# The order of two TensorE steps, convolution and second spread of B, in the middle stage of a vision network kernel

## The reference

```python
xw = windows_of_8x8(layernorm_over_channels(x)) + pos     # 64 steps, 64 channels
xz = seq @ W_in;  x, z = split(xz)                        # 128 + 128 channels
x  = silu(causal_conv1d(x, conv_w, 4 taps) + conv_b)
dt, B, C = split(x @ W_xproj)                             # 4, 16, 16 columns
dt = softplus(dt @ W_dt + b_dt)
h  = exp(dt * A) * h + dt * u * B      # scan over 64 steps, 128 channels x 16 states
y  = (h * C summed over states) + u * Dp
out = (y * silu(z)) @ W_out
```

## Time and profile before

| what | value |
|---|---|
| median of 3 runs | 8367.6 us |
| profiled execution | 8380.57 us |
| its span | 8378.7 us |
| VectorE busy, share of span | 81% |
| GpSimd busy | 62% |
| TensorE matmuls busy | 74% |
| ScalarE busy | 52% |
| granted TensorE clock, mean | 0.83 of full |

### The profile page before, as it was taken

The page is one execution under the profiler, slowest core; times in us unless marked ns, Lnnn a source line. Parts: engine busy times, 40 slices in busy tenths (PEclk is TensorE's granted clock), DMA queues, the critical chain, the costliest instruction groups (busy, mean ns, idle before and its releaser), DMA issues. The chain is left out here.

```text
span 8378.7 us, 102295 instructions
## 1 busy us (share of the span) xinstructions
PE 6196.3 (74%) x30542; PEld 2432.9 (29%) x30542; DVE 6788.1 (81%) x7950; ACT 4334.6 (52%) x5972; POOL 5194.6 (62%) x1732
## 2 busy tenths in 40 slices
PE   6888888888885777777777777777777777767737
PEld 3444444444441222222222222222222222222213
DVE  3555555555555999999999999999999999999976
ACT  1222222222223666666666666666666666666642
POOL 0000000000005999999999999999999999999950
PEclk8988898998986888888888888888888888888867
DMA  1111111111113556556556656655655665565567
GB/s 31 44 40 44 38 46 38 42 42 40 44 37 133 191 190 210 199 190 206 200 189 203 207 189 200 206 190 192 205 200 189 203 207 189 198 208 191 187 165 261
DMA packets 514970, 1253.48 MB, mean 150 GB/s; under 512 B 170313, under 2 KB 172525, under 8 KB 513901
## 3 DMA queue, kind: packets, MB, share of 16 engines
q1 hardware_dynamic: 514092, 1249.20, 45.8%
q10 hardware_dynamic: 320, 3.21, 0.2%
q0 software_dynamic: 512, 0.53, 0.0%
HBM read 943.30 MB, written 231.21 MB: 140 GB/s over the span
## 5 line engine op out<-in xcount | busy, mean ns | idle before, releaser
L1186 DVE TENSOR_TENSOR_SCAN b_h<-b_a,b_h 128x448 f32<-128x448 f32 x3584 | 3668.0, 1070 | 101.0 <-ACT b_a L1115 94.7
L1024 POOL TENSOR_TENSOR b_h<-b_h,b_ct 128x1792 f32<-128x1792 f32 x896 | 3570.3, 3987 | 278.4 <-DVE b_h L1186 265.6
L1115 ACT ACTIVATE b_a<-b_dts,decay 128x441 f32<-128x441 f32 x3584 | 2225.7, 629 | 1587.5 <-DVE b_h L1186 1560.0
L1036 POOL MEMSET b_seq<- 128x938 f32 x2 | 1.7, 880 | 2497.0 <-POOLq L799 2497.0
L1176 DVE TENSOR_TENSOR b_h<-b_dus,b_b 128x896 f32<-128x896 f32 x1344 | 1429.9, 1064 | 62.4 <-DMA b_dus<-d_dtu 61.1
L1283 PE MATMUL b_b<-b_rows,spread_b 16*128 16x512 f32 (+1 forms) x1792 | 565.2, 651 | 891.1 <-DVE b_h L1176 890.1
L1010 POOL TENSOR_TENSOR b_h<-b_dus,b_bt 128x896 f32<-128x896 f32 x448 | 933.3, 2083 | 44.6 <-DMA b_bt<-d_rows 27.8
L1291 PE MATMUL b_y<-b_h,fold 128*32 128x512 f32 (+1 forms) x7168 | 953.5, 659 | 8.1 <-POOL b_h L1024 8.1
L496 DVE TENSOR_TENSOR a_xg<-a_xd,a_pb 128x784 f32<-128x784 f32 x512 | 495.0, 967 | 511.7 <-PE a_pb L610 509.6
L1252 PE MATMUL b_w<-b_seq,w_conv 128*128 128x384 f32 (+1 forms) x896 | 560.1, 789 | 12.6 <-DMA b_seq<-b_seq 12.6
L1244 PE MATMUL b_w<-b_u,wx 128*64 128x512 f32 x448 | 361.3, 962 | 211.2 <-DVE b_dt L1208 211.2
(11 more groups left out here) (226 smaller groups left out, 8470.1 us busy)
## 6 DMA issues: line engine op xcount, KB each, us to landing
b_bt<-d_rows SPq DMA_DIRECT2D x448, 448.0 KB, 5.9
b_ct<-d_rows SPq DMA_DIRECT2D x448, 448.0 KB, 3.9
b_dts<-d_dt SPq DMA_DIRECT2D x448, 448.0 KB, 5.7
b_dus<-d_dtu SPq DMA_DIRECT2D x448, 448.0 KB, 6.3
a_xd<-a_xn SPq DMA_DIRECT2D x256, 196.0 KB, 3.4
d_dt<-b_dt SPq DMA_DIRECT2D x112, 448.0 KB, 2.5
d_dtu<-b_soft SPq DMA_DIRECT2D x112, 448.0 KB, 2.6
b_seq<-b_seq SPq DMA_DIRECT2D x112, 234.0 KB, 6.5
```

The lines of the kernel that those rows point to most:

```text
L1024: nc.gpsimd.tensor_tensor(two, two, ct[t // 4 % 2][:].unsqueeze(1).broadcast_to([P, 2, TB]), ALU.mult).then_inc(hc_done, 2)
L1115: a(steps(bank(aa, k)), steps(half(dts[t % 4], k)), ACT.Exp, scale=decay[:, t % 4, t // 4:t // 4 + 1]).then_inc(a_done, 1)
L1186: v.tensor_tensor_scan(half(hh[t], k), bank(aa, k), half(hh[t], k), 0.0, ALU.mult, ALU.add).then_inc(h_done, 1)
```

## The change

In TensorE's list for a unit, `spread_row(1, i, it)` moves from ahead of `conv` to behind it. Nothing else changes: the same instructions with the same waits on other engines, in all 112 units (the last has no `conv`).

```diff
@@ -1334,9 +1334,9 @@
                                 norm_end(spot(0, "var", it, kind), it + 1)
                             if finals:
                                 final_end(spot(1, "var2", it, kind), it - 1)
-                            spread_row(1, i, it)
                             if more:
                                 conv(spot(i, "conv", it, kind), 1 - i, it + i)
+                            spread_row(1, i, it)
                             if not first:
                                 fold_row(3, tile_no(i, 15, it) - UNIT)
                             if more:
```

## The result

The changed kernel takes 8373.2 us, the median of 20 runs, against 8362.5 for the kernel before in 20 runs beside them; the ratio is 1.0022 with an interval of 1.0011 to 1.0032. By the ratio that is some 18 us (the two medians differ by 10.7), where I had forecast 168. The profiled execution has a span of 8388.2 us, 9.5 more than before.

A forecast was written before the change was run, and what follows sets the result against it. VectorE was taken to set the time, busy 4984.8 of 5240 us. Later products, 80 us in unit 0 and 77 in unit 1, plus 11 for idling made 168: 8367.6 + 168 = 8535 us, range 8450 to 8640.

The forecast's parts named there:

- The late start: On TensorE, the convolution, now first, waits for ScalarE's logarithm: starts 0.12 us later in unit 1, 0.61 in unit 0.
- The stall moves from the product to inputs(5), and one replaces the other: On VectorE, inputs(5) stalls 2.3 us in unit 1 and 2.5 in unit 0; the old wait before the product goes.
- The sum for a given length of the pair: Gated product, if it waited before, comes 1.24 us plus late start later: 1.4 used for unit 1, 1.85 for unit 0.
- my own sign that the clock was the story: VectorE's new wait before inputs(5), expected at 2.3 to 4 us, being under 1 us would show the forecast wrong.
- I take the mix as it is.: TensorE's clock in spread and convolution: pair lengths stay mixed as before (4.26, 5.95 or 7.58 us); forecast chance 0.72.
- The adjustment for longer idling: In unit 0, TensorE idles 0.6 us longer before the convolution; half of 12 short pairs become usual: 11 us more.
- The other waits stay.: VectorE's waits besides the product's, such as 86.4 us for decays and 40.7 for dt*u by DMA, remain.
- The rival "faster": Convolution first ends TensorE's idle time and runs at the high clock in nearly every unit: -55 us, 8313; chance 0.05.
- within 0.3%: Whole kernel's time within about 0.3% (25 us) of no change; chance 0.04.
- the bounds of the clock term: Spread and convolution in TensorE: all pairs at 4.26 us gives about -55 us in total, all at 7.58 gives +310.

The follow-up runs named there:

- e1_late: Kernel before, old order, with the second spread also made to wait for ScalarE's logarithm as the convolution does; ratio to before 1.0080.
- e2_fill128: Kernel before, old order, plus eight 128-row matmuls of zeros ahead of the second spread to fill TensorE's idle time; ratio to before 0.9942.
- e3_fill16: Kernel before, old order, plus eight matmuls of zeros using only 16 rows ahead of the second spread; ratio to before 1.0019.
- e7_fill_center: Kernel before, old order, plus 128-row fillers ahead of the spread (eight in unit 0, twelve in unit 1) and eight ahead of unit 0's first strip; ratio 0.9907.
- e9_after_fill_center: Changed kernel plus 128-row fillers ahead of the convolution (eight in unit 0, twelve in unit 1) and eight ahead of unit 0's first strip; ratio to before 0.9888.
- e6_after_fill12: Changed kernel plus 128-row fillers ahead of the convolution, eight in unit 0 and twelve in unit 1; ratio to before 0.9938.

## Why the prediction was wrong, step by step

- *The late start.* Right. The pair starts 0.05 us after the logarithm, and 0.61 and 0.24 us after inputs(3) ends on average, where the two units that I had worked from gave 0.67 and 0.17.
- *The stall moves from the product to inputs(5), and one replaces the other.* Right in mechanism. In the stretch the wait before the product is gone in all of the units, and the new wait occurs 106 times.
- *The sum for a given length of the pair.* Right. For a middle pair it gave products 9.6 and 9.1 us after inputs(3) (the start of 0.67 or 0.17, then 5.95, 0.05 for the hand-over and 2.96); the changed kernel's middle pairs have 9.59 in unit 0 and 9.23 in unit 1. Its short ones have 8.10 and 7.61, where the same sum with 4.26 gives 7.9 and 7.4. The new wait agrees too: 2.4 and 2.3 us at middle pairs, where I had 2.5 and 2.3, but 0.9 and 0.65 at short ones. A wait under 1 us was my own sign that the clock was the story, and over half of the units show it.
- *"I take the mix as it is."* Wrong, and this is the step that failed. The pair's mean length fell from 5.57 to 4.59 us in unit 0 and from 6.76 to 5.55 in unit 1. Over 55 units each, 0.98 and 1.21 us are 120 us of the 168. With the 24 us of decays below, that leaves some 24 of the forecast, beside the 22 of the waits. I had argued that most of what TensorE does before the pair is unchanged. What it does first after the idle time was not: the convolution with 128 rows in place of the spread with 16. e1_late, e2_fill128 and e3_fill16 together show that this and not the moment of the start decides: the late start alone makes pairs longer, the 128-row filler makes them short and in the same order the 16-row filler of nearly the same duration does next to nothing.
- *The adjustment for longer idling*, +11 us, had the wrong sign: of unit 0's pairs 12 had been short, I took 6 for the changed kernel, and 41 were. It fits e1_late better, with 8.
- *"The other waits stay."* Wrong for the decays. Of their 86.4 us 34.5 went; I had counted 10 (the scan behind the product). The rest is in the main the wait behind unit 0's first strip, 64 us before and 43 after. That the clock in this strip sets that wait is what e7_fill_center and e9_after_fill_center show, in either order: a filler ahead of the strip takes it from 43 to 10 us in the old order and from 48 to 8 in the new. Why the strip meets the high clock more often once the pair has changed was not tried.
- *The rival "faster".* Its mechanism was the real one, and I gave it 0.05. Its price, with every pair short, was -55 us; e6_after_fill12, where every pair is short, is 0.6% faster than before, some 50 us. That kernel has fillers besides, so it bears the bound out only roughly. The real kernel lies between that bound and my sum, since 45 of its 104 pairs still meet the low clock.
- *The chances.* The measured ratio, 1.0022, is inside "within 0.3%", which I gave 0.04. The range began at 8450 though the bounds of the clock term that I had worked out reached 8313. It should have held them.

The row that should have warned me is the earlier trace rows read with the earlier trace rows: TensorE had been at work for 1.05 us, in the spread, when its clock fell. That left open whether the spread holds the clock up at all, and the change takes just that work out of first place. The Trainium skill, "TensorE: Matmul & The Clock Gate", Part 1 (The HAM clock gate), says that the gate follows how busy TensorE has recently been; the runs agree for matmuls of 128 rows (e2_fill128, where a record of the convolution takes 612 ns instead of 786) and differ for matmuls of 16 rows, which the profile counts as busy and which in the old order held next to nothing up (e3_fill16, 778 ns).

What stays open: how the number of rows enters (only 16 and 128 were tried, with zero weights in the fillers), why the 16-row filler seems to do more in the changed order than in the old one, and why unit 1 of the changed kernel still has 10 long pairs.

## What to carry to other kernels

A step whose duration depends on TensorE's clock has no fixed cost: before its old duration is carried into a new order, ask what TensorE does in the moments before it in the new order, and let the range hold both clock levels. When a stretch after an idle time is on the critical path, begin it with full-array work, or fill the gap with some; here sixteen records of zeros in unit 0 and twenty-four in unit 1, 2 to 3 us, made nearly every following pair short. And when a wait vanishes, read the next two in the list: here decays, then a transfer, took back part of each gain.

## What the runs showed of the hardware

- Matmuls that use 16 of the 128 rows, 2.05 us of them filling an idle time, left the clock of the next convolution about where it was in the old order (778 ns a record against 786 without them), while 1.95 us of 128-row matmuls brought its records to 612 ns, and to 559 with half as many again in unit 1. In the changed order the convolution's records took 665 and 660 ns without a filler, 622 with 16 rows and 573 with 128.
- Zeros suffice: the weights of the filler were all zero, and the clock stayed up all the same (1.00 through filler, spread and convolution in the unit of e2_fill128 shown).
- The two matmuls of the spread, rows 0 to 15 and 32 to 47 of their operands, take 1.12 us at the high clock and 2.07 at the low one.
